# Feed-forward of a hybrid layer in units of 512 columns instead of 1024, each batch in two passes

## The reference, cut to what matters

```python
z      = layernorm(x)                                     # over the 128 features
logits = mean(z, axis=tokens) @ w_gate + b_gate           # one choice per batch
top_vals, top_idx = top_k(softmax(logits), 2)             # 2 of 8 experts
y      = alpha * (gelu(z @ W1m + b1m) @ W2m + b2m)        # the dense network, 128 -> 512 -> 128
y     += (1 - alpha) * sum over the 2 chosen of share * (gelu(z @ W1e + b1e) @ W2e + b2e)
x      = x + y
```

## Time and profile before

| | us |
|---|---|
| median of 3 runs | 1385.68 |
| lowest and highest run | 1381.11, 1390.2 |
| the profiled execution, its own time | 1391.36 |
| span of its trace | 1389.4 |
| mean granted clock of TensorE | 0.915 |

### The profile page before, as it was taken

The page is one execution under the profiler, slowest core; times in us unless marked ns, Lnnn a source line. Parts: engine busy times, 40 slices in busy tenths (PEclk is TensorE's granted clock), DMA queues, the critical chain, the costliest instruction groups (busy, mean ns, idle before and its releaser), DMA issues. The chain is left out here.

```text
span 1389.4 us, 17492 instructions
## 1 busy us (share of the span) xinstructions
PE 1071.3 (77%) x5850; PEld 393.9 (28%) x5850; DVE 742.7 (53%) x1012; ACT 975.3 (70%) x884; POOL 325.7 (23%) x194
## 2 busy tenths in 40 slices
PE   4748777777799956777446888888888888679996
PEld 3213333333344422332341111111111111134443
DVE  5869998987566648998481001200300300256664
ACT  3767665754688832221336999999999999658885
POOL 3117776766111114665100000000000000011110
PEclk8769999999899978998777999999999999879998
DMA  2000100100100000000001111111111111000002
GB/s 73 0 16 30 31 30 30 60 30 31 32 30 30 31 24 0 0 0 1 8 0 33 24 24 32 37 24 28 22 33 34 24 24 28 11 31 31 30 30 61
DMA packets 24188, 36.48 MB, mean 26 GB/s; under 512 B 7362, under 2 KB 11970, under 8 KB 24130
## 3 DMA queue, kind: packets, MB, share of 16 engines
q1 hardware_dynamic: 24130, 35.71, 9.5%
HBM read 16.82 MB, written 6.29 MB: 17 GB/s over the span
## 5 line engine op out<-in xcount | busy, mean ns | idle before, releaser
L1674 ACT ACTIVATE att_prob<-att_s_ps 128x1536 f32<-128x1536 f32 x342 | 459.2, 1912 | 7.4 <-PE att_s_ps L1588 7.3
L1603 PE MATMUL att_o_ps<-att_prob,att_va 128*32 128x512 f32 x2048 | 273.9, 607 | 0.5 <-ACT att_prob L1674 0.5
L1705 DVE COPY att_o_sb<-att_o_ps 128x512 f32<-128x512 f32 x32 | 22.1, 691 | 381.7 <-PE att_o_ps L1603 381.7
L1588 PE MATMUL att_s_ps<-att_q_st,att_k_st 32*128 32x512 f16 x1024 | 134.4, 388 | 80.8 <-ACT att_prob L1674 76.1
L685 POOL TENSOR_TENSOR scan_hc<-scan_state,scan_c_rep 128x1024 f32<-128x1024 f32 x64 | 151.9, 2392 | 71.9 <-DVE scan_state L642 71.7
L787 POOL TENSOR_TENSOR ffn_veps<-ffn_mv,all_eps 128x4 f32<-128x4 f32 x16 | 9.1, 570 | 575.3 <-DVE ffn_mv L944 575.3
L642 DVE TENSOR_TENSOR_SCAN scan_state<-scan_decay,scan_drive_ps 128x1024 f32<-128x1024 f32 x64 | 142.9, 2270 | 0.3 <-ACT scan_decay L615 0.3
L282 PE MATMUL scan_y_ps<-scan_hc,all_ident 128*128 128x512 f32 x256 | 130.2, 634 | 8.3 <-DVE scan_y_sb L661 6.2
L1588 PEld LDWEIGHTS att_s_ps<-att_q_st,att_k_st 32*128 32x128 f16 x1024 | 33.1, 91 | 327.2 <-ACT att_prob L1674 315.9
L619 ACT ACTIVATE scan_c_rep<-scan_c_ps 128x1024 f32<-128x1024 f32 x64 | 65.4, 1022 | 80.4 <-PE scan_c_ps L282 80.1
L1012 DVE SCALAR_TENSOR_TENSOR ffn_hid_lo<-ffn_hid,ffn_share,ffn_hid_hi 128x1024 f16<-128x1024 f32 x64 | 81.9, 1283 | 48.8 <-ACT ffn_hid_hi L920 48.1
(11 more groups left out here) (215 smaller groups left out, 1505.8 us busy)
## 6 DMA issues: line engine op xcount, KB each, us to landing
ffn_w_sel<-w_split SPq DMA_DIRECT2D x16, 512.0 KB, 3.2
w_split<-scan_w_parts SPq DMA_DIRECT2D x8, 512.0 KB, 2.9
att_q_st<-hv_part SPq DMA_DIRECT2D x64, 64.0 KB, 2.1
att_k_st<-hv_part SPq DMA_DIRECT2D x64, 64.0 KB, 2.1
ln_x_half<-in_x SPq DMA_DIRECT2D x8, 256.0 KB, 2.8
scan_w_raw<-in_w1e SPq DMA_DIRECT2D x8, 256.0 KB, 3.2
scan_w_raw<-in_w2e SPq DMA_DIRECT2D x8, 256.0 KB, 3.4
out<-store_out SPq DMA_DIRECT2D x8, 256.0 KB, 2.4
```

Source lines behind the costliest of these rows:

```text
L1588: last = pe.matmul(s_ps[e % 2][:, n, :], k_st[rows, g % 2, kc * P:(kc + 1) * P], q_st[rows, g % 2, HALVES[half]], start=True, stop=True)
L1603: last = pe.matmul(o_ps[half][32 * j:32 * j + 32, :], va[:, g % 2, kc, j, :], prob[:, (GH * v + j) % RING, :], start=kc == 0, stop=kc == K ...
L1674: act.activation(prob[:, first % RING:first % RING + n, :], s_ps[e % 2][:, 0:n, :], ACT.Exp).then_inc(exped.sem, 1)
```

## The change

`ffn` is replaced by `mixture(t, name, jobs, rets)`, called with all four batches as `jobs` and nothing as `rets`. (`mixture` can also carry retention work between the units. With `rets` empty none of that is issued, and it is left out below.) What it does:

- A unit has 512 columns. A batch is `RUN` = 24 units: first the 12 of its first half, then the 12 of its second. Up and down are 3 matmuls each. PE still runs down two units behind up.
- Gelu, high part and low part are instructions of 512 columns. `hid` has three buffers, `hid_hi` and `hid_lo` four.
- The output of a half (`y` of 512 columns) is made by ACT (`output`) instead of DVE, and POOL adds 512 columns at a time.
- The layernorms of batches 1, 2 and 3 all lie in the units of batch 0 and shortly after: they begin at units 1, 9 and 17. Their second half follows three units behind the first. `share`, `bias`, `be` and the gate's small buffers have a place for each batch.
- PE transposes x straight from `t.x_t`; the copies to `x_half` are gone. There is one bank for transposed x (`a_ps`) and one for transposed z (`z_ps`), so that the second half of a layernorm begins after the first is normalised.
- SP reads both choices first, loads both biases, then the weights.
- All units are written out; there is no loop. Semaphores that started at a credit start at zero.
- Every stage clears its semaphores on POOL when it ends.

```diff
     def __exit__(self, *a):
+        nums = sorted(sem.num for sem in self.sems)
+        for first in (n for n in nums if n - 1 not in nums):
+            end = next(n for n in range(first, first + len(nums) + 1) if n not in nums)
+            self.nc.gpsimd.sem_clear(range(first, end))
         return self.ctx.__exit__(*a)
...
-def ffn(t, name):
+def mixture(t, name, jobs, rets):
...
+    M = 3 * FC
+    LAG = 2
+    RUN = 2 * M
+    norm_at = [(FIRST, "ffn", 0)] + [(1 + 8 * i, "ffn", i + 1) for i in range(N - 1)]
...
+        hid = sb("hid", [P, 3, HALF])
+        hid_hi, hid_lo = sb("hid_hi", [P, 4, HALF], F16), sb("hid_lo", [P, 4, HALF], F16)
...
+            @block.sync
+            def _(sp):
+                for i in range(N):
+                    sp.wait_ge(gate_steps.sem, gate_steps.at(i, 2))
+                    sp.sem_inc(loading, 1)
+                    chosen = [sp.value_load(which[0:1, i, k:k + 1], min_val=0, max_val=E - 1) for k in range(2)]
+                    for k, e in enumerate(chosen):
+                        sp.dma_start(be[:, i, k, :], d["be"][e]).then_inc(be_loaded[i], 16)
+                    for k, e in enumerate(chosen):
+                        if i:
+                            sp.wait_ge(downed.sem, downed.at(i - 1, M + (k + 2) * FC - 1))
...
+            @block.tensor
+            def _(pe):
+                def up(s):
+                    i, half, m, k, c = place(s)
+                    if m == 0:
+                        pe.wait_ge(z_rest.sem, z_rest.at(i, half))
+                    if k and c == 0:
+                        pe.wait_ge(e_loaded[k - 1], 16 * (i + 1))
+                    if s >= 2:
+                        pe.wait_ge(gelued.sem, gelued.at(0, s - 2))
+                    parts(h_ps[s % 2][:, :], weights(k, 0, 0, c), weights(k, 0, 1, c), z_hi[:, i, HALVES[half]],
+                          z_lo[:, i, HALVES[half]], True, True).then_inc(upped.sem, 1)
+
+                def down(s):
+                    i, half, m, k, c = place(s)
+                    if m == 0 and s:
+                        pe.wait_ge(y_made.sem, y_made.at(0, s // M - 1))
+                    pe.wait_ge(rested.sem, rested.at(0, s))
...
+                for h in range(2):
+                    turn_x(0, "ffn", 0, h)
+                    turn_z(0, h)
+                gate(0, 0)
+                for s in range(LAST + 1):
+                    if s < RUN * N:
+                        up(s)
+                    if s == 1:
+                        spread_shares(0)
+                    if 0 <= s - LAG < RUN * N:
+                        down(s - LAG)
+                    for q, kind, i in norms(s, 0):
+                        turn_x(q, kind, i, 0)
+                    for q, kind, i in norms(s, 3):
+                        turn_z(q, 0)
+                        turn_x(q, kind, i, 1)
+                    for q, kind, i in norms(s, 6):
+                        turn_z(q, 1)
...
+            @block.scalar
+            def _(act):
+                def gelu(s):
...
+                    act.activation(hid[:, s % 3, :], h_ps[s % 2][:, :], ACT.Gelu_apprx_tanh, bias=b1,
+                                   scale=1.0 / WS).then_inc(gelued.sem, 1)
+                    act.wait_ge(gelued.sem, gelued.at(0, s))
+                    if s >= 4:
+                        act.wait_ge(downed.sem, downed.at(0, s - 4))
+                    act.activation(hid_hi[:, s % 4, :], hid[:, s % 3, :], ACT.Copy,
+                                   scale=weight_of_expert(i, k)).then_inc(casted.sem, 1)
+
+                def output(s):
...
+                    act.activation(y[:, :], o_ps[:, :], ACT.Identity, bias=bias[:, i, 2:3],
+                                   scale=1.0 / WS).then_inc(y_made.sem, 1)
...
+                for s in range(LAST + 1):
+                    if s >= M + LAG and (s - LAG) % M == 0 and s - LAG <= RUN * N:
+                        output(s - LAG - 1)
+                    if s < RUN * N:
+                        gelu(s)
+                    for q, kind, i in norms(s, 3):
+                        high_part(q, kind, i, 0)
+                    for q, kind, i in norms(s, 6):
+                        high_part(q, kind, i, 1)
...
+            @block.vector
+            def _(dve):
+                for h in range(2):
+                    statistics(0, h)
+                    normalise(0, h)
+                    low_part(0, "ffn", 0, h)
+                choose(0)
+                share_rows(0)
+                for s in range(LAST + 1):
+                    if s < RUN * N:
+                        rest(s)
+                    if s == 1:
+                        take_shares(0)
+                    if s % RUN == 5 and s < RUN * N:
+                        output_bias(s // RUN)
+                    for q, kind, i in norms(s, 0):
+                        statistics(q, 0)
+                    for q, kind, i in norms(s, 1):
+                        normalise(q, 0)
+                    for q, kind, i in norms(s, 3):
+                        statistics(q, 1)
+                    for q, kind, i in norms(s, 4):
+                        low_part(q, kind, i, 0)
+                        normalise(q, 1)
+                    for q, kind, i in norms(s, 7):
+                        low_part(q, kind, i, 1)
...
-        ffn(t, "ffn1")
+        mixture(t, "ffn1", list(range(B)), [])
...
-        ffn(t, "ffn2")
+        mixture(t, "ffn2", list(range(B)), [])
```

More of the change, by code:

```diff
@@ L90, in sem @@
     def sem(self, name):
[L91 removed]
+        self.sems.append(self.ctx.enter_context(self.nc.semaphore(f"{self.name}_{name}")))
+        return self.sems[-1]
     def count(self, name, per=1, start=0):
@@ L714, in weights @@
         def weights(k, w, part, c):
             return (t.dense, *w_sel)[k][:, w, part, c * P:(c + 1) * P]
-        def weight_of_expert(k):
-            return share[:, k - 1:k] if k else t.blend[:, 0:1]
-        w_sel = [s.sb(f"w_sel{k}", [P, 2, 2, F], F16) for k in range(2)]
-        be = [s.sb(f"be{k}", [P, FC + 1]) for k in range(2)]
-        bias = s.sb("bias", [P, 3])
-        hid = s.sb("hid", [P, 2, T])
-        hid_hi, hid_lo = s.sb("hid_hi", [P, 3, T], F16), s.sb("hid_lo", [P, 3, T], F16)
@@ L726, in ffn @@
-        y = s.sb("y", [P, T])
-        h_ps = [s.ps(f"h_ps{k}", [P, T]) for k in range(2)]
-        o_ps = s.ps("o_ps", [P, T])
-        tok_ps, z_ps = (s.ps(n, [P, HALF]) for n in ("tok_ps", "z_ps"))
-        def x_place(b, k):
-            return (tok_ps, z_ps if isinstance(b, int) and b == 0 else tok_ps)[k]
-        def z_place(b, k):
-            return h_ps[0][:, HALVES[k]] if isinstance(b, int) and b == 0 else (z_ps, tok_ps)[k]
-        x_staged = s.count("x_staged", 2)
-        turned = s.count("turned", 2, 2)
@@ L765, in _ @@
             def _(sp):
-                with sp.Fori(0, B) as b:
-                    sp.wait_ge(gate_steps.sem, gate_steps.at(b, 2))
-                    for k in range(2):
-                        sp.wait_ge(downed.sem, downed.before(b, (k + 2) * FC - 1, M))
-                        sp.sem_inc(loading, 1)
-                        e = sp.value_load(which[0:1, k:k + 1], min_val=0, max_val=E - 1)
+                for i in range(N):
[7 more added lines that the diff above has]
+                            sp.wait_ge(downed.sem, downed.at(i - 1, M + (k + 2) * FC - 1))
+                            sp.sem_inc(loading, 1)
@@ L792, in body @@
-                def body(b, last):
-                    if not last:
-                        for k in range(2):
-                            deviation(b + 1, k)
-                    pool.wait_ge(y_made.sem, y_made.at(b))
-                    pool.sem_inc(seen, 1)
-                    pool.tensor_tensor(t.x_t[:, b, :], t.x_t[:, b, :], y[:, :], ALU.add).then_inc(added.sem, 1)
-                for k in range(2):
-                    deviation(0, k)
-                with pool.Fori(0, B - 1) as b:
-                    body(b, False)
@@ new lines, in add, with weigh @@
+                def add(s):
+                    i, half, m, k, c = place(s)
+                    pool.wait_ge(y_made.sem, y_made.at(0, s // M))
+                    x = t.x_t[:, jobs[i], HALVES[half]]
+                    pool.tensor_tensor(x, x, y[:, :], ALU.add).then_inc(added.sem, 1)
+                def weigh(r, w):
+                    h, n = divmod(w, HD)
+                    pool.wait_ge(scanned.sem, scanned.at(r, w))
+                    if n == 0:
+                        pool.wait_ge(copied.sem, copied.at(r, 4 * h + 2))
+                    if r or h:
+                        pool.wait_ge(summed.sem, summed.at(r, w // 4 - 2))
+                    pool.tensor_tensor(qm[:, n, :], mem[:, n, :], q_sb[:, HALVES[h]], ALU.mult).then_inc(weighed.sem, 1)
@@ new lines, in _ @@
+                for h in range(2):
+                    deviation(0, h)
+                for s in range(LAST + 1):
+                    if s >= M + LAG and (s - LAG) % M == 0 and s - LAG <= RUN * N:
+                        add(s - LAG - 1)
```

(10 more changed lines are left out.)

555 lines of the change are left out of this document (312 added, 243 removed).

## The result

| | before | after |
|---|---|---|
| median, us | 1385.51 | 1418.74 |
| lowest and highest, us | 1381.11, 1390.2 | 1417.45, 1419.48 |
| ratio, 95% interval | | 1.0238, 1.0204 to 1.0273 |
| span of the profiled execution, us | 1389.4 | 1417.7 |
| ffn1, ffn2, barrier to barrier in the trace, us | 156.3, 156.8 | 172.3, 172.8 |

The change made the kernel 33 us slower; forecast were 31 (1416, range 1397 to 1438). The two feed-forward stages took 32.0 us more. The stages that the change does not touch moved too: the one with retention was 3.4 us shorter, the one after it 1.6 shorter, attention 1.2 longer. In experiments 6 and 7, which have the old feed-forward, the first was 4.5 and 2.2 shorter, the second 1.4 and 1.6 shorter, attention 1.1 and 1.8 longer. So these shifts come without the change too, and I don't count them as its effect.

What follows compares the result with a forecast made beforehand. PE bounds the kernel before; ACT was to take over. Per stage, head +3.2, first to last gelu +15.9 and tail -3.8 make +15.3 us, twice +30.6, so the median goes from 1385.7 to 1416, range 1397 to 1438.

Steps and rivals of the forecast that it cites:

- The core step: Feed-forward units: ACT's instructions do not halve, so ACT becomes the bound at 1.41 us per half unit, above PE's 1.295.
- The pace: Batches 1 to 3: a gelu starts every 1.41 us, so 71 half units to the last gelu take 100.1 us.
- Batch 0: First gelu to gelu 24, all three layernorms included: PE rules and the stretch takes 43.6 us.
- six turns: Batch 0: PE waits 0.5 us at each turn of z, 3.0 in all, bounds 0 and 9.
- Rival (c): Waits in batch 0 decide: six turns wait 2.0 us each, +9 per stage more, 1434 in all; chance 0.12.
- Head: Start of each feed-forward stage: first gelu at 365.2 instead of 362.05, +3.2 us per stage.
- Tail: Last gelu to the end of the addition: 5.3 us instead of 9.1, -3.8 per stage.
- Outputs in batches 1 to 3: Six outputs left cost 0.59 us each on ACT and some 0.29 for a late up: 5.3 per stage.
- (a): Rival: PE stays the bound because ACT's pair fits into 1.295 us; 1400 in all; chance 0.15.
- my sign of being right: Batches 1 to 3: PE idles some 0.1 us per half unit, while gelus start every 1.41 us without ACT idle before.
- (b): Rival: not slower, as ACT halves truly (1.13 us) and deeper rings swallow every wait; 1379 in all; chance 0.06.
- (d): Rival: short idle spells drop TensorE's clock to 1.2 GHz, half units take 2.59 us, 1586 in all; chance 0.03.

Runs made afterwards that it cites:

- experiment 6: The kernel before the change, with only the clearing of semaphores at each stage's end added: 1385.41 us, ratio 1.0006.
- experiment 7: The kernel before the change, with only ACT's loop over the feed-forward's batches written out: 1381.53 us, ratio 0.9968.
- experiment 5: The changed kernel without the gelu's bias and with the high part's scale a constant 0.5, so neither has an operand per partition: 1407.59 us, ratio 1.0165.

## Why the prediction was right, and where two of its terms were off

**The core step held.** ACT's instructions did not halve: 722 ns was forecast for the high part and 722 measured, 684 for the gelu and 671 to 675 measured. ACT became the bound in batches 1 to 3; experiment 5 shows it by relieving ACT and landing on PE's pace.

**The pace was too dear, 1.41 for 1.33.** Bounds were 1.13 and 1.50. The part from high part to gelu was 0.63, as forecast. The part from gelu to high part was 0.70, not 0.78. I had carried over the 0.10 that the dependent pair cost beyond the whole gelu in the earlier trace rows; here it costs 0.03. The trace of before could have warned me: its pairs have both values, 1.21 from start to start in the earlier trace rows and 1.15 at 397.00 and 398.15 (experiment 7). Of its 96 pairs 42 stand at 0.03 and 54 at 0.09. I had read one value of two and taken it for the cost. Seventy-one times 0.08 would be 5.7, and the 71 gelus took 4.9 less than forecast.

**Batch 0 was too cheap, 43.6 for 50.0.** PE's own work was right: 31.1 + 7.6 = 38.7 forecast (three times 2.5 is 7.5, a slip of 0.1), 39.3 busy in the window. The waits were wrong. I took 3.0 for six turns and 0.9 for the output; PE idled 10.6, of which 7.9 at the turns, 1.3 each. I had set the chain of 4.1 us against three steps of 1.3 counted from PE's turn of x, and left out that DVE comes to its entry 2 us after that. The bounds I gave (0 and 9) held it. Rival (c) had this mechanism, at 2.0 each; what it lacked as well was the place where DVE stands. ACT's tanh, 5.3 us in two waits, was in no term of mine.

**The two errors have opposite signs** (-4.9 and +6.4 per stage), and 2 x 1.5 of them is left. That is luck: the total is better than its parts were: 16.0 per stage measured, 15.3 forecast.

**The small terms.** Head +2.6 for +3.2: the table load starts right behind the tanh at 363.44, where I had it behind the up at 363.8 (362.3 + 1.5), and the rest is the start of the up, at 362.01. Tail 5.15 for 5.3. Outputs in batches 1 to 3: the gelus around one are 1.90 and 1.66 us apart instead of twice 1.33, 0.90 for the 0.88 taken. Two table loads at gelus in place of six, eight instructions of output per stage, clears at nothing (experiment 6): as forecast. The load of 1.28 from 363.44 is followed by the gelu at 364.73; the drain behind a load, by which the Trainium skill (ScalarE: Activation LUTs, "What ACT_TABLE_LOAD costs") would add 1.4 per stage, does not show here either.

**The rivals.** (a), PE stays the bound, fell, though by 0.035 us only; I had put ACT's excess at 0.115, and PE's idle time of 0.1 per half unit, my sign of being right, does not show in the windows. (b) fell: the high part took 722 ns, not half of 1149. (d) did not come, but its condition hardly did either: PE's pause in a pure half unit is 0.03 us. There were longer ones, the waits of 1.3 us each for six turns of z and one of 1.7 for `y` in batch 0, and the granted clock from 367 to 415 was 1.00. So this trace does not show what the Trainium skill (TensorE: Matmul & The Clock Gate, "A second HAM failure mode: psum-queue depth-cycling") warns of, at least for pauses like these.

**What stays open.** What makes a dependent pair on ACT cost 0.03 or 0.09 us, and why the retention stage differs between executions by up to 4.5 us (160.8 to 165.3).

## What to carry to other kernels

Halving an instruction halves only the part that scales with columns; on ACT 0.17 us stay for a copy and 0.07 to 0.09 for each operand per partition (experiment 5), so look at the engine that is second before cutting, and at whether it has room for that. When a chain runs over several in-order engines by a table of steps, count its length in time from where each engine stands, not from the step's number: DVE reached its step 2.0 us after PE's, one and a half units, and about two steps more per hop were worth most of 14.5 us. Before taking a rewrite whole, look for its parts that need nothing else of it: loops written out, a copy dropped and a split tail gave 8.8 us to the kernel before, while the half units, with their steps put right, gave none. Read a change in one stage from that stage's length in the profile as well as from the total: here the other stages moved by up to 4.5 us on their own.
